# Product-key lookup layer: second-half maxima written to PSUM, candidate sums with one PSUM operand

## The reference, cut to what matters

```python
q = (xn @ w_q.T).reshape(b, s, 2, NH, KD).transpose(2, 0, 1, 3, 4)   # NH = 8 heads, two halves
sim = jnp.einsum('pbnhd,hkpd->pbnhk', q, keys_p)                     # 2 x 32 keys per head
scores, idx = jax.lax.top_k(sim, K)                                  # K = 8 of each half
all_scores = (scores[0][..., :, None] + scores[1][..., None, :]).reshape(b, s, NH, K * K)
all_idx = (idx[0][..., :, None] * NK + idx[1][..., None, :]).reshape(b, s, NH, K * K)
sc, pk = jax.lax.top_k(all_scores, K)
indices = jnp.take_along_axis(all_idx, pk, axis=-1)
wd = down[indices]
hmid = jnp.einsum('bnd,bnhkd->bnhk', inputs, wd)
hmid = jax.nn.sigmoid(sc) * jax.nn.gelu(hmid, approximate=False)
wu = up[indices]
return jnp.einsum('bnhk,bnhkd->bnd', hmid, wu)
```

## Time and profile before

| what | us |
|---|---|
| median of 3 runs (lowest to highest) | 1605.89 (1604.61 to 1609.22) |
| the profiled execution, its own time | 1600.34 |
| its span in the trace | 1598.5 |
| DVE busy in the span | 1023.4 (64%) |
| PE busy in the span | 1406.6 (88%) |
| POOL's pair sums, L1773 | 240.2 in 128 instructions |
| DVE's gatings, L1846 | 158.4 in 128 instructions |
| ACT's sigmoids, L1748 | 129.6 in 128 instructions |

### The profile page before, as it was taken

One profiled execution on the slowest core, in us unless ns is written; L12 is line 12 of the kernel. 1 busy time (PEld: TensorE's weight loads), 2 busy tenths in 40 slices (PEclk: granted clock), 3 DMA queues, 4 the chain that ended last, 5 costly groups with the idle time before them and its releaser, 6 DMA issues.

```text
span 1598.5 us, 30106 instructions
## 1 busy us (share of the span) xinstructions
PE 1406.6 (88%) x9483; PEld 945.5 (59%) x9497; DVE 1023.4 (64%) x3372; ACT 909.5 (57%) x1883; POOL 706.3 (44%) x1068
## 2 busy tenths in 40 slices
PE   5997789999998577887778987799899999998998
PEld 2544357777776466776754553444477777775543
DVE  5663467666775799999965553443476666765444
ACT  3665356666665477777746664423376666664321
POOL 5341144554453589989854330100164444542300
PEclk9999799999999599999899999799999999998999
DMA  2007000000000000000000000000000000000000
GB/s 68 18 21 287 1 5 7 3 3 3 3 3 1 27 1 1 1 0 0 1 1 1 1 1 1 27 1 0 3 5 4 3 3 3 3 1 1 1 14 13
DMA packets 12666, 21.78 MB, mean 14 GB/s; under 512 B 3088, under 2 KB 9120, under 8 KB 11936
## 3 DMA queue, kind: packets, MB, share of 16 engines
q1 hardware_dynamic: 12576, 20.63, 3.7%
HBM read 19.58 MB, written 1.05 MB: 13 GB/s over the span
## 4 chain that ended last, share of the span: by engine, by line
PE 68%; DVE 15%; ACT 9%; issue 6%; POOL 1%; DVEq 0%; DMA 0%; ACTq 0%; SPq 0%; POOLq 0%
PE bank L934 7%; PE bank L969 7%; PE bank L947 6%; DVE sb_both L1846 4%; PE bank L900 4%; PE bank L921 4%; PE bank L1879 3%; PE bank L2118 3%; PE bank L901 3%; PE bank L913 3%; PE bank L409 2%; PE bank L451 2%; ACT sb_KM L598 2%; ACT sb_both L598 2%; ACT bank L1748 2%
## 5 line engine op out<-in xcount | busy, mean ns | idle before, releaser
L1213 POOL TENSOR_TENSOR sb_both<-sb_both,sb_winv 128x512 f32<-128x512 f32 x256 | 260.9, 1040 | 292.4 <-DVE sb_winv L1143 292.4
L1036 ACT ACTIVATE sb_both<-sb_both,sb_wneg 128x256 f32<-128x256 f32 x512 | 253.0, 495 | 126.8 <-DVE sb_wneg L1137 126.8
L1773 POOL TENSOR_TENSOR sb_KM<-sb_OT 128x1024 f32<-128x1024 f32 x128 | 240.2, 1912 | 31.9 <-DVE sb_both L1846 27.9
L1677 PE MATMUL bank<-sb_ident,sb_both 128*128 128x128 f32 x1024 | 139.2, 286 | 60.8 <-DVE sb_both L1846 38.6
L1137 DVE CUSTOM_DVE_ANT_0 sb_both<-bank,sb_pen 128x256 f32<-128x256 f32 x512 | 182.1, 420 | 0.0
L1296 POOL TENSOR_TENSOR sb_ntmp<-sb_rstd 128x2 f32<-128x2 f32 (+2 forms) x123 | 24.1, 196 | 338.5 <-DVE sb_rstd L218 332.1
L1846 DVE SCALAR_TENSOR_TENSOR sb_both<-sb_KM,sb_best,bank 128x1024 f32<-128x1024 f32 x128 | 158.4, 1274 | 10.6 <-ACT bank L1748 10.4
L1677 PEld LDWEIGHTS bank<-sb_ident,sb_both 128*128 128x128 f32 x1024 | 118.8, 147 | 75.3 <-DVE sb_both L1846 48.9
L1748 ACT ACTIVATE bank<-sb_KM 128x1024 f32<-128x1024 f32 x128 | 129.6, 1023 | 36.4 <-DVE sb_both L1846 31.9
L947 PE MATMUL bank<-sb_ident,sb_both 128*128 128x128 f32 x1024 | 134.1, 273 | 8.7 <-DVE sb_QT L1150 5.9
L947 PEld LDWEIGHTS bank<-sb_ident,sb_both 128*128 128x128 f32 x1024 | 118.3, 141 | 27.2 <-issue 12.7
(11 more groups left out here) (282 smaller groups left out, 2769.3 us busy)
## 6 DMA issues: line engine op xcount, KB each, us to landing
sb_ctxT_in<-in_ctxT SPq DMA_DIRECT2D x24, 128.0 KB, 2.3
sb_F<-in_F SPq DMA_DIRECT2D x2, 1024.0 KB
sb_XO<-in_ctx SPq DMA_DIRECT2D x8, 128.0 KB, 2.0
sb_WKQ<-in_WKQ SPq DMA_DIRECT2D x1, 1024.0 KB, 9.0
sb_W1ALL<-in_ctxT SPq DMA_DIRECT2D x1, 1024.0 KB, 4.9
sb_xn_all<-in_keymask SPq DMA_DIRECT2D x1, 1024.0 KB, 4.5
out_x<-sb_x SPq DMA_DIRECT2D x4, 256.0 KB, 2.3
sb_x<-in_x SPq DMA_DIRECT2D x1, 896.0 KB, 5.0
```

Source lines behind the costliest of these rows:

```text
L1036: last = act.activation(p, p, ACT.Exp, scale=-1.0, bias=wneg[:, t % 4, h, i:i + 1], accum_out=wsum[:, t % 4, h, i:i + 1])
L1213: pool.tensor_tensor(p, p, winv[:, t % 4, :, i:i + 1].broadcast_to([P, 2, SEQ]), ALU.mult).then_inc(w_norm, 1)
L1677: last = pe.matmul(weight_bank(c), gated[:, h % 4, c * P:(c + 1) * P], ident[:], is_transpose=True, start=(h == 0 and c % 4 == 0), stop=(h ...
L1773: pool.tensor_tensor(dst, s[:, h, 0, :].unsqueeze(2).broadcast_to([P, NK, NK]), s[:, h, 1, :].unsqueeze(1).broadcast_to([P, NK, NK]), ALU. ...
```

## The change

The second halves' eight largest no longer go to `top` in SBUF but to 64 columns of a PSUM bank. For tile 0 that is bank 2 (`home` 2), for all others bank 0 (`home` 0). The candidates' sums take their first operand from there and their second, the first halves, from SBUF. The eight maxima of the first halves are issued first, then a small memset and the eight of the second halves.

Banks 0 and 1 are those of the even heads' sigmoids. Bank 0 is free between the gating of head 4 and the sigmoid of head 6. So ACT gets a new wait: the sigmoid of head 6 (except in the last tile) waits for the four candidates' sums of the next tile. In tile 0 the sigmoid of head 1, whose banks are 2 and 3, waits for the sums of tile 0.

```diff
-    top = sb("top", [P, 2, 16, TOPK])
+    top = sb("top", [P, 2, PK_HEADS, TOPK])
...
+    def second_tops(home):
+
+        return bank[home][:, 0:PK_HEADS * TOPK].rearrange("p (h k) -> p h k", h=PK_HEADS)
...
                     act.wait_ge(gated_ready, n - 1)
+                if first == 0 and h == 1:
+                    act.wait_ge(combos_done, len(BANDS))
+                if h == 6 and last_ > 0:
+                    act.wait_ge(combos_done, len(BANDS) * (i + 2))
                 act.activation(sig_bank(h), pairsum[:, h % 4, :], ACT.Sigmoid).then_inc(sig_ready, 1)
...
-            if lo == 0:
-                dve.wait_ge(sims_ready, i + 1)
-                S["own_wait"](dve)
-            for n in range(lo, hi):
-                dve.max(top[:, t % 2, n, :], sims[:, t % 4, n * NK:(n + 1) * NK]).then_inc(top_done, 1)
+            dve.wait_ge(sims_ready, i + 1)
+            S["own_wait"](dve)
+            for h in range(PK_HEADS):
+                dve.max(top[:, t % 2, h, :], sims[:, t % 4, 2 * h * NK:(2 * h + 1) * NK]).then_inc(top_done, 1)
+            if home == 0:
+                dve.wait_ge(gated_ready, PK_HEADS * (i - 1) + 5)
+                S["own_wait"](dve, 2)
+            for h in range(PK_HEADS):
+                dve.max(second_tops(home)[:, h, :], sims[:, t % 4, (2 * h + 1) * NK:(2 * h + 2) * NK])\
+                   .then_inc(top_done, 1)
...
-                dve.tensor_tensor(dst, pair[:, :, 0, lo:hi].unsqueeze(3).broadcast_to([P, PK_HEADS, hi - lo, n]),
-                                  pair[:, :, 1, 0:n].unsqueeze(2).broadcast_to([P, PK_HEADS, hi - lo, n]), ALU.add)\
+                dve.tensor_tensor(dst, second[:, :, 0:n].unsqueeze(2).broadcast_to([P, PK_HEADS, hi - lo, n]),
+                                  top[:, t % 2, :, lo:hi].unsqueeze(3).broadcast_to([P, PK_HEADS, hi - lo, n]), ALU.add)\
                    .then_inc(combos_done, 1)
```

More of the change, by code:

```diff
@@ L113, in build @@
         c15 = sb("c15", [P, TILES])
-        scratch = sb("scratch", [P, 2])
+        scratch = sb("scratch", [P, 4])
         rstd = sb("rstd", [P, TILES])
@@ L1797, in vector1, with tops, combine @@
         dve.tensor_tensor(bn_c[:], beta[:], bn_c[:], ALU.subtract).then_inc(bn_ready, 1)
-        def tops(i, t, lo, hi):
-            if lo == 0:
-                dve.wait_ge(sims_ready, i + 1)
-                S["own_wait"](dve)
-            for n in range(lo, hi):
-                dve.max(top[:, t % 2, n, :], sims[:, t % 4, n * NK:(n + 1) * NK]).then_inc(top_done, 1)
-        def combine(i, t):
+        def tops(i, t, home):
+            dve.wait_ge(sims_ready, i + 1)
[8 more added lines that the diff above has]
+                   .then_inc(top_done, 1)
+        def combine(i, t, home):
             dve.wait_ge(top_done, 16 * i + 16)
-            pair = top[:, t % 2].rearrange("p (h q) k -> p h q k", q=2)
+            second = second_tops(home)
             for lo, hi, n, at in BANDS:
                 dst = combos[:, :, at:at + (hi - lo) * n].rearrange("p h (a b) -> p h a b", b=n)
-                dve.tensor_tensor(dst, pair[:, :, 0, lo:hi].unsqueeze(3).broadcast_to([P, PK_HEADS, hi - lo, n]),
-                                  pair[:, :, 1, 0:n].unsqueeze(2).broadcast_to([P, PK_HEADS, hi - lo, n]), ALU.add)\
+                dve.tensor_tensor(dst, second[:, :, 0:n].unsqueeze(2).broadcast_to([P, PK_HEADS, hi - lo, n]),
+                                  top[:, t % 2, :, lo:hi].unsqueeze(3).broadcast_to([P, PK_HEADS, hi - lo, n]), ALU.add)\
                    .then_inc(combos_done, 1)
@@ L1854, in step @@
                     if last_ > 0:
-                        tops(i + 1, t + 1, 0, 16)
-                        combine(i + 1, t + 1)
+                        tops(i + 1, t + 1, 0)
+                        combine(i + 1, t + 1, 0)
                 if h == 5 and last_ > 0:
@@ L1860, in step @@
                     bests(i + 1, t + 1, 4, 8)
-        tops(0, 0, 0, 16)
-        combine(0, 0)
+        tops(0, 0, 2)
+        combine(0, 0, 2)
         bests(0, 0, 0, PK_HEADS)
```

## The result

The change made the kernel slower: 1621.94 us (1618.42 to 1628.02) against 1605.25 (1604.14 to 1609.22), a ratio of 1.0114 with a 95% interval of 1.0091 to 1.0137. That is +16.7 us, where 30.1 were forecast; it lies inside the range of 1612 to 1647, near its lower end. The profiled execution took 1618.42 with a span of 1616.6, 18.1 us above the span before.

A forecast was written before the change was run, and what follows sets the result against it. POOL waits for DVE, so DVE's tile in the lookup layer was taken as the bound. Terms -24.8 + 1.5 + 33.0 + 20.4 = +30.1 us on 1605.9 gave 1636 us, 1.9% slower, range 1612 to 1647.

The forecast's parts named there:

- The sums come free: DVE's candidates' sums no longer stand until POOL's sums end: -24.8 us over 15 tiles (bounds -23.0 and -26.6).
- A surcharge for the PSUM operand: Rival: each DVE sum pays a fixed 62 extra cycles for reading PSUM, total 1640 us; chance 0.07.
- The rival that the sums are not freed: POOL still holds DVE's sums because one operand comes from SBUF; about 1661 us, chance 0.04.
- Maxima: DVE's maxima keep number and size; an added memset and wait on DVE's own gating cost at most +1.5 us.
- The sigmoid's wait: ACT's sigmoid 6 and the gelus and table loads behind it move behind the sums: +33.0 us (31.5 to 34.5).
- G to S: On DVE, from start of head 5's gating to start of head 7's: forecast 5.90 us, was 3.70.
- PE's clock: PE's longer pause before head 7's transposes lowers its clock, DVE waits: +20.4 us (bounds -5.9 to +28.0).
- The rival of an unchanged clock: PE's clock stays about as it is, only the first three terms hold: 1616 us (1610 to 1621), chance 0.18.
- The faster case: ACT between sums and head 7's gating: if the wait adds nothing, POOL bounds, 23 us gained, 1583; chance 0.06.

The follow-up runs named there:

- x1: Kernel before plus only ACT's new wait ahead of head 6's sigmoid, maxima and sums still in SBUF: 1644.21 us, ratio 1.0272.
- x2: The change with second maxima in bank 7; PE's second down-projection half waits for the sums instead of ACT's sigmoid 6: 1582.1 us, ratio 0.9878.
- x4: The change plus 20 transposes of zeros on PE behind those of head 6, result unaltered: 1609.58 us, ratio 1.0052.

## Why the prediction was right in its direction and too high in its size

*The sums come free:* forecast -24.8 us, measured 33.84 - 7.74 = -26.1. Right; four in a row take 0.52, a little less than the 0.60 chosen. A surcharge for the PSUM operand does not show: the median is 180 ns with either source, and four sums in a row take 0.52 with a PSUM operand and 0.53 with both in SBUF where POOL does not hold them (the tile of x1 in the last section). So the rule of the Trainium skill ("VectorE: DVE Perf Modes", section "The TRN2 errata") that was weighed there does not show in these instructions, and that rival falls. The rival that the sums are not freed falls with the longest sum, 225 ns.

*Maxima:* forecast +1.5. From the first maximum to the sums it was 1.62 before (643.69 to 645.31) and 1.65 after (632.75 to 634.40): 15 x 0.03 = +0.5. The memset and the wait on DVE's own work all but vanish.

*The sigmoid's wait:* forecast G to S 5.90, +33.0 us; measured 5.91 in the tile above and 2.25 more than before on average, 15 x 2.25 = +33.7. Right, and x1 shows by adding the wait alone that it is the cause; x2, where the wait is gone together with the old bank, has 4.31.

*PE's clock:* forecast +20.4, measured 18.2 - 5.9 = +12.3. This is the term that was mis-sized. The mechanism held: the clock fell in all twelve tiles that were read, and x4 gave the time back. The weights came out near as well: nine of the twelve at 0.81 or 0.82 and three at 0.90, where two in three and one in three were taken. What was too high is the price of a tile. The nine waited 1.28 to 1.96 us for PE, 1.70 on average, where 2.42 was taken from the one tile at 0.72, a clock that no tile after had; the three waited 0.44 or 0.45 where 0.80 was taken. Over 14 tiles that is 18.2 / 14 = 1.30 us a tile instead of 1.88. The pause itself was 2.68 us where 3.3 were worked out, because PE's transposes of heads 3 to 6 closed up into one run of 3.66 us, whose end came 4.57 behind G instead of 3.94. Whether the shorter pause is why the price was lower was not tested.

These measured terms add up to -26.1 + 0.5 + 33.7 + 12.3 = +20.4 us; the layer's 14 tiles grew by 14 x (18.18 - 16.70) = 20.8. The profiled span grew by 18.1: outside the 14 tiles the trace after is 2.7 us shorter, in parts that differ by more than that between the kept traces. The median grew by 16.7. So of the 13.4 us that the forecast was too high, about 8 are the clock's term; what lies between the sum of the measured terms and the median, 3.7 us, comes from no term of the forecast and was not followed.

The rival of an unchanged clock reached up to 1621 us by its own count, a hair below the measured time, but its premise was wrong. x4 is close to what it described: 1.0052 x 1605.9 = 1614, between its 1616 and the 1610 that it gave for a clock that never falls. The faster case named the right place: with ACT's chain out of the way x2 gained 1602.65 - 1582.1 = 20.6 us, where it gave 23. Its chance was counted unevenly at the end of the prediction: half of 0.06 is 0.03 for a faster kernel, not 0.05.

## What to carry to other kernels

A buffer that is idle in one engine's view is lent at the price of a wait on the engine that owns it; read what is queued behind that wait in the owner's order before looking at the wait itself. Here the borrowed bank turned 2.2 us of hidden gelus and table loads per tile into path, while another bank, where the next writer, PE, waited only 0.67 us for the sums in the tile shown, turned the same saving into 1.2% of the whole kernel. When a stage gets a new pause on PE, price the lower clock from the tiles that already show one, but from several of them: here the one worst tile was priced at 2.42 us, and the tiles that came cost 1.70 and 0.44.

## What the runs showed of the hardware that was not expected

Twenty transposes of zeros per tile made the program faster than leaving PE idle: the granted clock of the tiles rose from between 0.81 and 0.90 to 1.00 in eleven of twelve, the mean tile went from 18.18 to 16.97 us, and 10 to 12 us of the whole came back, with PE busy 14.12 us of 16.80 instead of 14.34 of 18.50.

What POOL's hold costs depends on when DVE arrives: with the wait alone (x1) the same SBUF sums were held 22.94 us in all instead of 33.84, though nothing about them was altered. Two of its tiles show it, POOL's row of sums first in each pair:

```profile
600.94 7.53 POOL L1775 TENSOR_TENSOR sb_KM<-sb_OT 128x1024 f32<-128x1024 f32 x4 [0.76 <-DVE sb_both L1848]
606.78 2.08 DVE L1814 TENSOR_TENSOR sb_QT<-sb_top 128x64 f32<-128x64 f32 x4
...
659.22 7.52 POOL L1775 TENSOR_TENSOR sb_KM<-sb_OT 128x1024 f32<-128x1024 f32 x4 [0.86 <-DVE sb_both L1848]
666.66 0.53 DVE L1814 TENSOR_TENSOR sb_QT<-sb_top 128x64 f32<-128x64 f32 x4
```

In the first, POOL's row ends at 608.47 and DVE's four sums, begun at 606.78, end 0.39 behind it. In the second POOL ends at 666.74, 0.08 behind the start of DVE's sums, and the four take 0.53 us.
